# Attention masks on tiles of TensorE's array, shorter runs for the stack loads, late weights in pairs

## The chip, the cores and the metric

The kernel runs on one core of a Trainium2 chip. The time is the device time of one execution in microseconds, which is the time of the slowest core and here of the only one. TensorE (PE) multiplies, VectorE (DVE), ScalarE (ACT) and GpSimd (POOL) work on tiles, and SyncE (SP) issues nearly all transfers between memory (DRAM) and the on-chip memory (SBUF).

## The reference

A gated cross-attention block and a gated mixture of experts over 32 batches of 128 tokens with 128 features:

```python
x = x + tanh(g_xattn[0]) * attention(layernorm(x), ctx, ctx, mask, Wq, bq, ..., bo)
x = x + tanh(g_ffn[0]) * experts(layernorm(x), Wg, bg, Wt, bt, W1, b1, W2, b2)
# attention: 16 heads of 8 features
scores = einsum('bhqd,bhkd->bhqk', q, k) / sqrt(8)
scores = where(mask[:, None, :, :], finfo.min, scores)   # mask [b, q, k], one for all heads
out = softmax(scores) @ v @ Wo.T + bo
# experts: 8, all computed for every token
gate = softmax(x @ Wg + bg); thr = sigmoid(x @ Wt + bt) / 8
w = max(gate - thr, 0); w = w / sum(w)
out = sum_e w[:, e] * (gelu(x @ W1[e] + b1[e]) @ W2[e] + b2[e])
```

## The kernel before, in words

The kernel has two stages. The expert stage is the longer one and isn't part of the change. In the attention stage the 32 batches are handled in 16 groups of two. A loop written out over turns (`it`) works on several groups at once: `group_at(it, ahead)` tells which group a step handles in this turn, so that a turn holds the natural scores of group `it`, the transposed scores of the second batch of group `it - 1`, the head sums of that group, and so on. Each engine has its own program with the same turns, and its order is the order in which the code is written. Engines wait for each other by semaphores.

**Scores.** Queries and keys are kept in fp32 parts, stored to DRAM (`kq_scratch`) and read back as stacks (`kq_st`): four strips of 32 rows of the array (`ROWS`), each with 24 rows for one head at a time. For each batch TensorE makes the scores twice. The natural ones (queries on partitions, L1000) give DVE the row maxima (`neg_max`, L727). The maxima are turned by TensorE (max0 for the first batch, max1 for the second), copied by ACT (`maxT`) and sent by SP into two more rows of the stacks (L410, L418). The transposed ones (keys on partitions, L1025) then have the maxima taken off and go to ACT's exponentials (`probs`, L567). The values product (L1047) follows, with 32 columns of the array for each of four heads.

**Masks.** The mask of a batch, 128 x 128 bytes, is loaded as words with queries on partitions (`mask_words`, L360) and cast by POOL to bf16 (`mask_b`, L513). A matmul with a diagonal matrix of -2^126 (`masked_ident`) adds it to the scores: with the diagonal as weights for the natural ones (L983), with the mask as weights for the transposed ones (L1011). Each is a full matmul of 128 rows and 512 columns, that is one bank of PSUM with four heads. A batch has four banks each way. The masks of two banks make a pair, and the pair ends with the semaphore for which DVE or ACT waits; in the natural way banks 2 and 3 come first, then 0 and 1.

**After the values.** ACT copies the head sums (`headsT`), TensorE turns them, DVE divides (`merged`), TensorE turns again, ACT copies (`mergedT`), and the projection `wo` (L1124) follows. L1145 to L1147 are the projections to keys and queries, L1191 to L1193 those to values, L1204 the gate.

**SP's queue.** In a turn SP issues, in this order and each behind its own waits: the max1 rows (L410), the next mask and context (L360, L365), four stack loads of 192 KB (L377), the max0 rows (L418), expert weights and x (L386, L391), and four stores of keys and queries (L399, L403). In turn 0 `later_weights` adds six small loads behind that.

Of the kernel before, what the change touches and what calls it, by code (L numbers as in the profile page):

```python
# [85 lines left out]
def gated_block(nc, a):  # L86
# [3 lines left out]
    with ctx:  # L90
# [33 lines left out]
        mask_words = sa("mask_words", [P, 2, GB, S // 4], I32)  # L124
        mask_b = sa("mask_b", [P, 2, GB, S], BF16)
# [23 lines left out]
        merged = sa("merged", [P, 2, GB * H, HD], F32)  # L149
        mergedT = sa("mergedT", [P, 2, GT], F32)  # L150
# [4 lines left out]
        x2n = sa("x2n", [P, 2, GB, D], F32)  # L155
# [34 lines left out]
        kq_dram = nc.dram_tensor("kq_scratch", (NG, ROWS * 24, SLABS * 2 * GT), F32)  # L190
# [9 lines left out]
        bv_in = sem("bv_in")  # L200
        bias_in = sem("bias_in")
# [69 lines left out]
        N_WTS = 6 * 16  # L271
# [34 lines left out]
        def wait_spare_loads(eng):  # L306

            for u in range(2):
                eng.wait_ge(ctx_in[u], 8 * NG)
                eng.wait_ge(mask_in[u], 8 * NG)  # L310
                eng.wait_ge(w_in[u], 8 * NG)
# [10 lines left out]
        def _(sp):  # L322
            ctx_v = a["ctx"].rearrange("(g b p) d -> g p b d", p=P, b=GB)
            mask_v = a["mask"].rearrange("(g b) q k -> g q b k", b=GB)
# [13 lines left out]
            sp.dma_start(mask_words[:, 0, :, :], mask_v[0]).then_inc(mask_in[0], 16)  # L338
# [3 lines left out]
            def later_weights():  # L342

                sp.dma_start(bo_row[:], a["bo"].partition_broadcast(P)).then_inc(wts_in, 16)
                sp.dma_start(wo_sb[:], a["woT"]).then_inc(wts_in, 16)
                sp.dma_start(wg_sb[:], a["wg"]).then_inc(wts_in, 16)
                sp.dma_start(bg_row[:], a["bg"].partition_broadcast(P)).then_inc(wts_in, 16)
                sp.dma_start(b1_sb[:], a["b1"]).then_inc(wts_in, 16)
                sp.dma_start(b2_sb[:], a["b2"]).then_inc(wts_in, 16)

            def rows_of(g, c):
                return kq_dram[g].rearrange("(r c d) (s x) -> c (d s) r x", r=ROWS, c=3, s=SLABS)[c]
# [52 lines left out]
            def body(it):  # L405
# [19 lines left out]
                elif it == 0:  # L425
                    later_weights()
# [912 lines left out]
```

## Time and profile before

| | us |
|---|---|
| median of 3 runs | 620.04 (617.59 to 621.89) |
| the profiled execution: its time | 622.03 |
| its span in the trace | 620.2 |

| engine | busy us | share |
|---|---|---|
| PE | 593.7 | 96% |
| DVE | 479.4 | 77% |
| ACT | 378.2 | 61% |
| POOL | 178.8 | 29% |

### The profile page before, as it was taken

How to read it: one execution, taken by the hardware profiler on the slowest of the kernel's cores; microseconds unless marked ns; L12 is line 12 of the kernel's file. 1: busy time of each engine (PE TensorE's matmuls, PEld its weight loads, DVE VectorE, ACT ScalarE, POOL GpSimd, SP SyncE). 2: the span in 40 equal slices, each digit the busy share in tenths (PEclk: the TensorE clock that was granted, in tenths of full speed). 3: DMA queues.
4: the chain of work that ended last, by engine and by line, in shares of the span. 5: the costliest groups of instructions: out<-in, count | busy, mean ns of one | idle time of the engine just before them, and what ended most of it. 6: DMA issues, size and time to landing. Idle time of an engine off the chain costs nothing.

```text
span 620.2 us, 13793 instructions
## 1 busy us (share of the span) xinstructions
PE 593.7 (96%) x4504; PEld 451.6 (73%) x4504; DVE 479.4 (77%) x940; ACT 378.2 (61%) x625; POOL 178.8 (29%) x224
## 2 busy tenths in 40 slices
PE   7888999999999998999999999999999999999998
PEld 6655666666666655788878788787887887887886
DVE  3464777777777766588788889888888888888886
ACT  3143555555655545867776767676777676776773
POOL 7523444454552221212203212212112112122121
PEclk9997999999999989999999999999999999999999
DMA  6765654555655420051111211121121121121210
GB/s 184 200 157 139 177 176 146 143 162 159 164 150 160 144 55 5 6 103 51 45 58 35 66 58 52 51 65 42 45 68 51 36 65 51 51 64 38 68 51 17
DMA packets 43998, 55.12 MB, mean 89 GB/s; under 512 B 9520, under 2 KB 27824, under 8 KB 42416
## 3 DMA queue, kind: packets, MB, share of 16 engines
q1 hardware_dynamic: 43504, 53.99, 30.8%
q8 instruction: 29, 0.48, 0.3%
q10 hardware_dynamic: 448, 0.53, 0.2%
q14 instruction: 17, 0.14, 0.1%
HBM read 39.16 MB, written 14.81 MB: 87 GB/s over the span
## 4 chain that ended last, share of the span: by engine, by line
PE 85%; ACT 4%; DVE 3%; DMA 2%; SPq 2%; issue 2%; ACTq 0%; DVEq 0%
PE ps_h L1069 10%; PE ps_h L1071 9%; PE ps_h L1070 9%; PE ps_y L1084 9%; PE ps_y L1086 9%; PE ps_y L1085 9%; PE misc L1047 5%; PE scores L983 5%; PE scores L1011 3%; PE scores L1000 3%; PE scores L1025 3%; ACT probs L567 2%; PE misc L1124 2%; PE misc L1216 1%; PE misc L974 1%
## 5 line engine op out<-in xcount | busy, mean ns | idle before, releaser
L591 ACT ACTIVATE h_sb<-ps_h,b_sb 128x512 f32<-128x512 f32 x256 | 175.9, 689 | 102.2 <-PE ps_h L1071 92.2
L750 DVE TENSOR_TENSOR h_low<-h_sb,h_high 128x512 fp32r<-128x512 f32 x256 | 164.6, 683 | 0.1
L530 POOL TENSOR_TENSOR yT<-yT,weighted 128x512 f32<-128x512 f32 x54 | 70.8, 1311 | 277.8 <-DVE weighted L925 277.8
L746 DVE CAST h_high<-h_sb 128x512 fp32r<-128x512 f32 x128 | 97.8, 764 | 52.6 <-ACT h_sb L591 52.4
L727 DVE TENSOR_REDUCE neg_max<-scores 128x8 f32<-128x1024 f32 x64 | 78.0, 1222 | 48.0 <-PE scores L983 48.0
L1069 PE MATMUL ps_h<-x_high,w_high 128*128 (+1 forms) x256 | 101.8, 398 | 2.1 <-ACT h_sb L591 2.0
L1084 PE MATMUL ps_y<-h_high,w_high 128*128 128x512 f32 x256 | 100.2, 391 | 0.3 <-ACT h_high L595 0.3
L1071 PE MATMUL ps_h<-x_high,w_low 128*128 (+1 forms) x256 | 99.8, 390 | 0.0
L1070 PE MATMUL ps_h<-x_low,w_high 128*128 (+1 forms) x256 | 99.7, 390 | 0.0
L1086 PE MATMUL ps_y<-h_high,w_low 128*128 128x512 f32 x256 | 99.7, 389 | 0.0
L1085 PE MATMUL ps_y<-h_low,w_high 128*128 128x512 f32 x256 | 99.6, 389 | 0.0
L595 ACT ACTIVATE h_high<-ps_h,b_sb 128x512 fp32r<-128x512 f32 x128 | 87.2, 681 | 0.0
L567 ACT ACTIVATE probs<-scores 128x1024 f32<-128x1024 f32 x64 | 62.9, 1006 | 17.3 <-PE scores L1011 17.3
L1069 PEld LDWEIGHTS ps_h<-x_high,w_high 128*128 128x128 f32 x256 | 48.1, 188 | 14.6 <-issue 4.7
L1084 PEld LDWEIGHTS ps_y<-h_high,w_high 128*128 128x128 f32 x256 | 48.0, 188 | 11.2 <-ACT h_high L595 0.7
L1071 PEld LDWEIGHTS ps_h<-x_high,w_low 128*128 128x128 f32 x256 | 48.0, 188 | 10.2
L1086 PEld LDWEIGHTS ps_y<-h_high,w_low 128*128 128x128 f32 x256 | 48.0, 188 | 10.2
L1085 PEld LDWEIGHTS ps_y<-h_low,w_high 128*128 128x128 f32 x256 | 48.1, 188 | 9.8
L1070 PEld LDWEIGHTS ps_h<-x_low,w_high 128*128 128x128 f32 x256 | 48.1, 188 | 9.3
L925 DVE SCALAR_TENSOR_TENSOR weighted<-ps_y,b_sb,w_row 128x512 f32<-128x512 f32 x55 | 41.0, 746 | 0.0
L983 PE MATMUL scores<-mask_b,masked_ident 128*128 128x512 bf16 x128 | 39.2, 392 | 0.0
L1011 PE MATMUL scores<-masked_ident,mask_b 128*128 128x512 bf16 x128 | 35.8, 389 | 0.0
(127 smaller groups left out, 719.8 us busy)
## 6 DMA issues: line engine op xcount, KB each, us to landing
w_row<-w_scratch SPq DMA_DIRECT2D x64, 256.0 KB, 3.1
kq_st<-kq_scratch SPq DMA_DIRECT2D x64, 192.0 KB
kq_scratch<-kq_parts SPq DMA_DIRECT2D x30, 256.0 KB, 2.9
w_raw<-in_w_ffn SPq DMA_DIRECT2D x16, 256.0 KB, 2.9
kq_scratch<-kq_parts SPq DMA_DIRECT2D x32, 128.0 KB, 2.7
ctx_sb<-in_ctx SPq DMA_DIRECT2D x16, 128.0 KB, 3.2
out_y<-y_out SPq DMA_DIRECT2D x7, 256.0 KB, 2.3
x_all<-in_x SPq DMA_DIRECT2D x13, 128.0 KB, 3.5
```

What stands on the lines that cost most here:

```text
L567: nc.scalar.activation(probs[:, b, half * 8 * S:(half + 1) * 8 * S], scores[:, 2 + 2 * half:4 + 2 * half, :].rearrange("p r x -> p (r x)") ...
L591: nc.scalar.activation(h_sb[:, j % HBUF, :], ps_h[:, j % 4, :], ACT.Gelu_apprx_tanh, bias=b1_sb[:, j:j + 1]).then_inc(h_done, 1)
L595: nc.scalar.activation(h_high[:, j % HBUF, :], ps_h[:, j % 4, :], ACT.Gelu_apprx_tanh, bias=b1_sb[:, j:j + 1]).then_inc(high_even, 1)
L727: nc.vector.tensor_reduce(neg_max[:, b, rows, :], scores[:, rows, :].rearrange("p r (s k) -> p r s k", k=S), AX.X, ALU.max, negate=True).t ...
L746: nc.vector.tensor_copy(h_high[:, j % HBUF, :], h_sb[:, j % HBUF, :]).then_inc(high_odd, 1)
L750: nc.vector.tensor_tensor(h_low[:, j % HBUF, :], h_sb[:, j % HBUF, :], h_high[:, j % HBUF, :].bitcast(F32), ALU.subtract).then_inc(low2_do ...
L1069: mm(dst, w_high[:, e, cols], xh, start=True, stop=False)
L1070: mm(dst, w_high[:, e, cols], xl, start=False, stop=False)
L1071: mm(dst, w_low[:, e, cols], xh, start=False, stop=True).then_inc(h_full, 1)
L1084: mm(dst, w_high[:, E + e, cols], h_high[:, j % HBUF, :], start=(f == 0), stop=False)
L1085: mm(dst, w_high[:, E + e, cols], h_low[:, j % HBUF, :], start=False, stop=False)
L1086: mm(dst, w_low[:, E + e, cols], h_high[:, j % HBUF, :], start=False, stop=(f == FC - 1)).then_inc(w2_done, 1)
```

## The change

**Masks.** A DMA for each batch now loads the mask once into each of the four strips: partition i of a strip holds queries 4i to 4i+3 with 128 keys each (512 bytes). So that query order fits, the turned inputs, and headsT on the way back, are dealt (query 4i+j goes to place 32j+i). A natural pair is now eight matmuls, each of 32 rows and 32 columns of the array with 512 moving columns. A transposed pair is eight matmuls of 32 rows and 128 columns of the array with 128 moving columns. `mask_words` has one buffer in place of two, and its load moves from the turn two ahead to the turn one ahead. To make room, `merged`, `mergedT` and `x2n` have one buffer each.

**Matmuls without meaning.** `keep_busy` adds four full matmuls of 512 columns a turn; their results are overwritten.

**Transfers.** `kq_scratch` gets 16 words of padding behind each slab, so that a stack load reads four runs of 2 KB a row, where it read one of 8 KB. The six late weights come in three pairs, in turns 0, 2 and 6, with semaphores of their own.

```diff
-        mask_words = sa("mask_words", [P, 2, GB, S // 4], I32)
-        mask_b = sa("mask_b", [P, 2, GB, S], BF16)
+        mask_words = sa("mask_words", [P, GB, S], I32)
+        mask_b = sa("mask_b", [P, 2, GB, 4, S], BF16)
...
-        kq_dram = nc.dram_tensor("kq_scratch", (NG, ROWS * 24, SLABS * 2 * GT), F32)
+        kq_dram = nc.dram_tensor("kq_scratch", (NG, ROWS * 24, SLABS, 2 * GT + 16), F32)
...
+            def load_mask(g):
+                for b in range(GB):
+                    every = bass.AP(a["mask"].tensor, (g * GB + b) * 32 * S, [[0, ROWS], [S, 32], [1, S]])
+                    sp.dma_start(mask_words[:, b, :], every).then_inc(mask_in[g % 2], 16)
...
-            def later_weights():
...
+            def later_weights(it):
+                if it == 0:
+                    sp.dma_start(bo_row[:], a["bo"].partition_broadcast(P)).then_inc(wts_in, 16)
+                    sp.dma_start(wo_sb[:], a["woT"]).then_inc(wts_in, 16)
+                elif it == 2:
...
+                elif it == 6:
...
-                if (g := group_at(it, 2)) is not None:
-                    u = g % 2
+                if (g := group_at(it, 1)) is not None:
                     if g > 0:
-                        wait_count(sp, mask_done, g - 1)
-                        sp.dma_start(mask_words[:, u, :, :], mask_v[g]).then_inc(mask_in[u], 16)
+                        sp.wait_ge(mask_done, g)
+                        load_mask(g)
...
-                        sp.dma_start(kq_st[32 * r:32 * r + 24, g % 3, :, :, :].rearrange("p s n t -> p (s n t)").bitcast(F32),
-                                     kq_dram[g, 24 * r:24 * r + 24, :]).then_inc(kq_in[g % 3], 16)
+                        sp.dma_start(kq_st[32 * r:32 * r + 24, g % 3, :, :, :].rearrange("p s n t -> p s (n t)").bitcast(F32),
+                                     kq_dram[g, 24 * r:24 * r + 24, :, 0:2 * GT]).then_inc(kq_in[g % 3], 16)
...
-                    nc.gpsimd.tensor_copy(mask_b[:, u, :, :], mask_words[:, u, :, :].bitcast(U8)).then_inc(mask_done, 1)
+                    nc.gpsimd.tensor_copy(mask_b[:, u, :, :, :].rearrange("p b j k -> p b (j k)"), mask_words[:].bitcast(U8)).then_inc(mask_done, 1)
...
-                    nc.scalar.activation(headsT[:, 0, :], misc[:, bank_of("V0"), 0:2 * P], ACT.Copy).then_inc(misc_read[bank_of("V0")], 1)
+                    nc.scalar.activation(headsT[:, 0, :].rearrange("p (k i j) -> p k j i", k=2, j=4),
+                                         misc[:, bank_of("V0"), 0:2 * P].rearrange("p (k j i) -> p k j i", k=2, j=4), ACT.Copy).then_inc(misc_read[bank_of("V0")], 1)
...
-            def natural_mask(r, b, u):
-                return mm(scores[:, r, :].rearrange("p (s k) -> p s k", s=SLABS), masked_ident[:],
-                          mask_b[:, u, b, :].unsqueeze(1).to_broadcast([P, SLABS, S]), start=False, stop=True)
+            def keep_busy(bank, n, u):
+                for _ in range(n):
+                    mm(scores[:, bank, :], masked_ident[:], mask_b[:, u, 0, :, :].rearrange("p j k -> p (j k)"), start=True, stop=True)
+
+            def natural_mask(pair, b, u):
+                for j in range(4):
+                    for r in pair:
+                        rows = slice(32 * r, 32 * r + 32)
+                        ins = mm(scores[32 * j:32 * j + 32, r, :].rearrange("p (s k) -> p s k", s=SLABS), masked_ident[rows, rows],
+                                 mask_b[rows, u, b, j, :].unsqueeze(1).to_broadcast([32, SLABS, S]), start=False, stop=True)
+                return ins
...
-            def transposed_mask(r, b, u):
-                return mm(scores[:, 2 + r, :].rearrange("p (s q) -> p s q", s=SLABS), mask_b[:, u, b, :],
-                          masked_ident[:].unsqueeze(1).to_broadcast([P, SLABS, S]), start=False, stop=True)
+            def transposed_mask(pair, b, u):
+                for j in range(4):
+                    for r in pair:
+                        rows = slice(32 * r, 32 * r + 32)
+                        ins = mm(scores[:, 2 + r, :].rearrange("p (s j i) -> p j s i", s=SLABS, j=4)[:, j], mask_b[rows, u, b, j, :],
+                                 masked_ident[rows, rows].unsqueeze(1).to_broadcast([32, SLABS, 32]), start=False, stop=(j == 3))
+                return ins
...
+                if (g := group_at(it, 0)) is not None:
+                    wait_count(pe, tr_rest_read, 2 * g)
+                    keep_busy(5, 2, g % 2)
...
+                if (g := group_at(it, 0)) is not None:
+                    pe.wait_ge(nat_rest_read, 2 * g + 2)
+                    keep_busy(0, 1, g % 2)
...
+                if (g := group_at(it, 0)) is not None:
+                    keep_busy(0, 1, g % 2)
```

TensorE, the second half of a turn, before: the values product of the second batch (L1047), its rest of the natural masks (L983), the values projection, the transposed scores of the first batch (L1025) with their masks (L1011), the gate (L1204) and the turn of the head sums (L1216).

```order
L1047 MATMUL misc<-probs,v_pad 32x128 x16
L983 MATMUL scores<-mask_b,masked_ident 128x512 x2
L1191 MATMUL misc<-wv_high,inT_high 128x128
...
L1025 MATMUL scores<-kq_st 128x128 x16
L1011 MATMUL scores<-masked_ident,mask_b 128x512 x4
L1204 MATMUL misc<-wg_sb,x2T_sb 128x9 x2
L1216 MATMUL misc<-ident_sb,headsT 128x128 x4
```

The same piece in the changed kernel (L1009 and L1040 are the masks, L1002 is `keep_busy`):

```order
L1075 MATMUL misc<-probs,v_pad 32x128 x16
L1009 MATMUL scores<-mask_b,masked_ident 32x512 x8
L1002 MATMUL scores<-mask_b,masked_ident 128x512 x2
L1222 MATMUL misc<-wv_high,inT_high 128x128
...
L1055 MATMUL scores<-kq_st 128x128 x16
L1040 MATMUL scores<-masked_ident,mask_b 128x4x32 x16
L1002 MATMUL scores<-mask_b,masked_ident 128x512
L1240 MATMUL misc<-wg_sb,x2T_sb 128x9 x2
L1002 MATMUL scores<-mask_b,masked_ident 128x512
L1254 MATMUL misc<-ident_sb,headsT 128x128 x4
```

Two full masks became eight small ones, four became sixteen, and four full matmuls without meaning stand at three places of this half; the first half of the turn has none.

SP, from the stores of turn 0 to the max0 rows of turn 1, before:

```order
L403 DMA kq_scratch<-kq_parts 32x4x512 x2
L344 DMA bo_row<-in_bo 128x128
L345 DMA wo_sb<-in_woT 128x128
L346 DMA wg_sb<-in_wg 128x9
L347 DMA bg_row<-in_bg 128x9
L348 DMA b_sb<-in_b 128x32
L349 DMA b_sb<-in_b 128x8
L410 DMA kq_st<-maxT 4x4x128 x2
L360 DMA mask_words<-in_mask 128x2x32
L365 DMA ctx_sb<-in_ctx 128x2x128
L377 DMA kq_st<-kq_scratch 24x2048 x4
L418 DMA kq_st<-maxT 4x4x128 x2
```

The same stretch now:

```order
L413 DMA kq_scratch<-kq_parts 32x4x512 x2
L353 DMA bo_row<-in_bo 128x128
L354 DMA wo_sb<-in_woT 128x128
L420 DMA kq_st<-maxT 4x4x128 x2
L333 DMA mask_words<-in_mask 128x1x128 x2
L375 DMA ctx_sb<-in_ctx 128x2x128
L387 DMA kq_st<-kq_scratch 24x4x512 x4
L428 DMA kq_st<-maxT 4x4x128 x2
```

Four issues left the stretch, and one mask load became two.

## Rows read from the trace of the kernel before

**Rows 1.** Three turns as stretches: us, busy us (instructions) by engine, PEclk, DMA share, GB/s

```profile
35.39:52.31 16.92, 13.46 (x167) 8.48 (x167) 8.38 (x18) 6.22 (x11) 7.33 (x13) 0.87 0.57 137
...
52.31:66.87 14.56, 13.65 (x173) 8.88 (x172) 10.06 (x25) 6.86 (x12) 2.88 (x4) 0.92 0.52 140
...
121.63:135.29 13.66, 13.30 (x179) 8.91 (x179) 10.53 (x30) 7.55 (x14) 6.37 (x10) 1.00 0.56 160
```

**Rows 2.** TensorE's timeline in one settled turn: start us, us, operation, count [wait]

```profile
121.63 0.67 PE L1000 MATMUL scores<-kq_st 24*128 24x128 f32 x16
...
122.23 0.61 PE L983 MATMUL scores<-mask_b,masked_ident 128*128 128x512 bf16 x2
...
122.67 0.38 PE L974 MATMUL misc<-ident_sb,merged 128*128 128x128 f32 x2
...
123.62 0.68 PE L1124 MATMUL misc<-wo_sb,mergedT 128*128 128x128 f32 x4
...
124.23 1.08 PE L1047 MATMUL misc<-probs,v_pad 128*32 128x128 f32 x32
...
128.81 0.67 PE L1000 MATMUL scores<-kq_st 24*128 24x128 f32 x16 [0.28 <-ACT probs L567]
...
130.96 0.61 PE L983 MATMUL scores<-mask_b,masked_ident 128*128 128x512 bf16 x2
...
131.62 0.30 PE L1191 MATMUL misc<-wv_high,inT_high 128*128 128x128 f32 x1
...
133.00 1.04 PE L1011 MATMUL scores<-masked_ident,mask_b 128*128 128x512 bf16 x4
...
133.88 0.58 PE L1204 MATMUL misc<-wg_sb,x2T_sb 128*128 128x9 f32 x4
```

**Rows 3.** The same timeline, other engines

```profile
122.13 0.42 DVE L804 TENSOR_TENSOR merged<-misc,sums_r 128x256 f32<-128x256 f32 x1
...
123.09 0.38 ACT L610 ACTIVATE mergedT<-misc 128x256 f32<-128x256 f32 x1 [0.22 <-PE misc L974]
...
127.67 1.91 ACT L567 ACTIVATE probs<-scores 128x1024 f32<-128x1024 f32 x2
...
127.78 1.11 SPq L418 DMA_DIRECT2D kq_st<-maxT  x2
...
131.09 0.38 ACT L662 ACTIVATE headsT<-misc 128x256 f32<-128x256 f32 x1 [1.52 <-PE misc L1047]
```

**Rows 4.** Chain of waits that ends at 48.37: start us, us, what

```profile
34.73 0.43 SPq L346
...
36.37 0.43 SPq L349
...
39.15 1.75 SPq L377
...
42.74 5.59 DMA kq_st<-maxT
```

**Rows 5.** TensorE's timeline behind that chain

```profile
48.37 1.12 PE L1025 MATMUL scores<-kq_st 26*128 26x128 f32 x16 [2.79 <-DMA kq_st<-maxT]
```

**Rows 6.** Groups by line, settled turns: busy us, mean ns of one

```profile
L513 POOL CAST mask_b<-mask_words 128x256 bf16<-128x256 uint8 x11 | 4.4, 396 | 0.0
```

**Rows 7.** Instructions of one line: ns min/median/max, first and last start

```profile
L545 ACT ACTIVATE wqk_high<-probs x2: 438/442/447, 7.2 to 7.5; 128x128 fp32r<-128x128 f32 x2
```

**Rows 8.** Two stretches of 1 us, columns as in rows 1

```profile
127.00:128.00 1.00, 0.98 (x6) 0.39 (x5) 0.97 (x4) 0.59 (x3) 0.60 (x1) 1.00 0.69 164
...
134.00:135.00 1.00, 0.99 (x9) 0.78 (x8) 1.00 (x5) 0.67 (x1) 0.00 (x0) 1.00 1.01 383
```

**Rows 9.** One stretch, and TensorE's timeline in it

```profile
224.00:228.00 4.00, 3.22 (x50) 2.07 (x50) 1.23 (x1) 1.54 (x2) 3.53 (x5) 0.66 0.11 23
...
224.78 0.69 PE L1000 MATMUL scores<-kq_st 24*128 24x128 f32 x16 [0.92 <-ACT probs L567]
...
226.36 1.94 PE L1047 MATMUL misc<-probs,v_pad 128*32 128x128 f32 x32
```

More of the change, by code:

```diff
@@ L148, in gated_block @@
         sums_r = sa("sums_r", [P, GB * H], F32)
-        merged = sa("merged", [P, 2, GB * H, HD], F32)
-        mergedT = sa("mergedT", [P, 2, GT], F32)
+        merged = sa("merged", [P, GB * H, HD], F32)
+        mergedT = sa("mergedT", [P, GT], F32)
         x_biased = sa("x_biased", [P, GB, D], F32)
@@ L154, in gated_block @@
         rstd2 = sa("rstd2", [P, 2, GB], F32)
-        x2n = sa("x2n", [P, 2, GB, D], F32)
+        x2n = sa("x2n", [P, GB, D], F32)
         x2T = sa("x2T_sb", [P, 2, GT], F32)
@@ L556, in first_low_stores @@
             def first_low_stores():
-                rows = kq_dram[0].rearrange("(r c d) (s x) -> c (d s) r x", r=ROWS, c=3, s=SLABS)
+                rows = kq_dram[0].rearrange("(r c d) s x -> c (d s) r x", r=ROWS, c=3)[:, :, :, 0:2 * GT]
                 misc_wait_read(act, "kq", 0)
@@ L607, in body @@
                     misc_wait_full(act, "merged", g)
-                    if g >= 2:
-                        misc_wait_full(act, "wo", g - 2)
-                    nc.scalar.activation(mergedT[:, u, :], misc[:, bank_of("merged"), 0:GT], ACT.Copy).then_inc(misc_read[bank_of("merged")], 1)
+                    if g >= 1:
+                        misc_wait_full(act, "wo", g - 1)
+                    nc.scalar.activation(mergedT[:], misc[:, bank_of("merged"), 0:GT], ACT.Copy).then_inc(misc_read[bank_of("merged")], 1)
                 if (g := group_at(it, -3)) is not None:
@@ L661, in body @@
                         misc_wait_full(act, "heads", g - 1)
-                    nc.scalar.activation(headsT[:, 1, :], misc[:, bank_of("V1"), 0:2 * P], ACT.Copy).then_inc(misc_read[bank_of("V1")], 1)
+                    nc.scalar.activation(headsT[:, 1, :].rearrange("p (k i j) -> p k j i", k=2, j=4),
+                                         misc[:, bank_of("V1"), 0:2 * P].rearrange("p (k j i) -> p k j i", k=2, j=4), ACT.Copy).then_inc(misc_read[bank_of("V1")], 1)
                     if g == NG - 1:
@@ L801, in body @@
                     dve.wait_ge(recip_done, g + 1)
[L802 to L804 removed]
+                    if g >= 1:
+                        misc_wait_full(dve, "merged", g - 1)
+                    nc.vector.tensor_tensor(merged[:], hv[:, :, 0:HD], sums_r[:].unsqueeze(2).to_broadcast([P, GB * H, HD]),
                                             ALU.mult).then_inc(misc_read[bank_of("heads")], 1)
@@ L873, in body @@
                     dve.wait_ge(rstd2_done, g + 1)
-                    if g >= 2:
-                        misc_wait_full(dve, "x2T", g - 2)
+                    if g >= 1:
+                        misc_wait_full(dve, "x2T", g - 1)
                     for b in range(GB):
-                        nc.vector.tensor_scalar(x2n[:, u, b, :], x_all[:, g * GB + b, :],
+                        nc.vector.tensor_scalar(x2n[:, b, :], x_all[:, g * GB + b, :],
                                                 mean_var2[:, u, b, 0:1], rstd2[:, u, b:b + 1], ALU.subtract, ALU.mult).then_inc(x2n_done, 1)
@@ L973, in turn @@
                 for b in range(n):
-                    ins = nc.tensor.transpose(misc[:, k, b * S:(b + 1) * S], src(b), ident[:])
+                    out = misc[:, k, b * S:(b + 1) * S]
+                    ins = nc.tensor.transpose(dealt(out) if b >= GB else out, src(b), ident[:])
                 ins.then_inc(misc_full[k], 1)
@@ L1102, in body @@
                     misc_wait_read(pe, "heads", g)
-                    turn("merged", g, lambda b: merged[:, u, b * H:(b + 1) * H, :].rearrange("p h d -> p (h d)"))
+                    turn("merged", g, lambda b: merged[:, b * H:(b + 1) * H, :].rearrange("p h d -> p (h d)"))
                 if (g := group_at(it, -3)) is not None:
@@ L1108, in body @@
                         pe.wait_ge(g_copied, 1)
-                    turn("x2T", g, lambda b: x2n[:, u, b, :])
+                    turn("x2T", g, lambda b: x2n[:, b, :])
                     if g == NG - 1:
@@ L1123, in body @@
                     for b in range(GB):
-                        ins = mm(misc[:, bank_of("wo"), b * D:(b + 1) * D], mergedT[:, u, b * S:(b + 1) * S], wo_sb[:], start=True, stop=True)
+                        ins = mm(misc[:, bank_of("wo"), b * D:(b + 1) * D], mergedT[:, b * S:(b + 1) * S], wo_sb[:], start=True, stop=True)
                     ins.then_inc(misc_full[bank_of("wo")], 1)
```

50 lines of the change are left out of this document (23 added, 27 removed).

## The prediction

> **What bounds the kernel now.** I read the times by turn first (a turn is one step of the loop over groups), then TensorE's timeline in one settled turn, then the engines it waits for, and last the chain of waits in the one turn that is longer. A settled turn lasts 13.66 us, and TensorE is busy for 13.30 of it; DVE, ACT and POOL are busy for 10.53, 7.55 and 6.37 [rows 1]. There are 16 groups and some 15 such turns, and the expert stage behind them isn't touched. So the attention stage is TensorE's, with one exception: the turn from 35.39 to 52.31 lasts 16.92 us and the one behind it 14.56 [rows 1].
>
> Not all of TensorE's time counts. Its row at 128.81 shows a 0.28 us wait for ACT's exponentials, which run from 127.67 to 129.58 [rows 2, 3]. Projection `wo` starts at 123.62, just behind ACT's copy mergedT, which ends at 123.47; that copy follows the turn of `merged` (122.67), which itself follows DVE's product (it ends at 122.55) [rows 2, 3]. The values projection at 131.62 starts just behind ACT's headsT (ends at 131.47), though the masks before it began at 130.96 and need only 0.44 [rows 2, 3]. In those three places a quicker mask gives TensorE a longer wait, and no time.
>
> **Prices.** A pair of full mask matmuls takes 0.44 us (122.23 to 122.67), so one of 512 columns takes 0.22, and that is also the price of each matmul without meaning [rows 2]. A turn has eight such pairs, 16 matmuls.
>
> *Transposed pair, now 8 matmuls of 128 columns on two strips.* The nearest row is the sixteen products of kq_st on four strips, 0.60 us or 38 ns each (121.63 to 122.23), so 0.30 for eight [rows 2]. From below, four in a row on each strip at a quarter of 0.22 make 0.22. Those of kq_st load fp32 weights and the mask's are bf16, so I take 0.28.
>
> *Natural pair, now 8 matmuls of 512 columns on 32x32 tiles.* No row shows such tiles. The values product shows that column tiles do overlap: 32 matmuls in 1.08 us, 34 ns each [rows 2]. If each of the eight starts 38 ns behind the last, the pair takes 7 x 0.038 + 0.22 = 0.49; if they start together, 0.22 and a little. The start distances of both rows hold a weight load and a stream on one strip, which eight separate tiles don't share, so I take the middle, 0.36, and keep 0.25 and 0.49.
>
> The Trainium skill (TensorE: Matmul & The Clock Gate, "Measured speedup vs the span model") has tiles start 4 ns apart, which would make this pair 0.25; no row here shows that. The Trainium skill (TensorEngine Tiling (Array Packing), "Key Properties") also says that a change of the tiling mode drains TensorE. That speaks against the change, since every natural pair now enters and leaves a mode of its own; by it the pair goes to the upper end.
>
> **The sum for a turn.**
> - Rest of the natural masks for the second batch with two matmuls without meaning: 0.36 + 0.44 = 0.80, in place of the 0.66 from 130.96 to 131.62 in which 0.22 was waiting: +0.14.
> - Transposed masks of the first batch (133.00 to 133.88): 0.56 in place of 0.88: -0.32. The two meaningless matmuls around the gate: +0.44. The wait for nat_rest_read ahead of them costs nothing: DVE's second maximum follows the first, and TensorE has the values projection and 32 matmuls in between.
> - Next natural pair: -0.08.
> - Masks between `merged` and `wo`: 0, hidden by mergedT as above.
> - First transposed pair of the second batch: -0.16, since the max0 transpose, ACT's copy and its exponentials hang on it. The second pair: 0; the wait at 128.81 grows instead.
> - Natural pair behind the products at 128.81: -0.08.
>
> That is -0.06 a turn, -0.9 us over 15. What is saved in the masks goes into the four meaningless matmuls. With both upper prices it is about +0.3 a turn (+4.5), with both lower ones, where DVE's merged and ACT's exponentials stop some of it, -0.4 (-6).
>
> *Edits off the path.* POOL's cast of the mask has four times the elements, and 0.40 us for 256 [rows 6] makes at most 1.6 for 1024; POOL is busy for 6.37 of 13.66 us [rows 1] and hides it. If that cover went, SP would stand before the next mask load, with the stack loads and the max0 rows behind it. ACT's headsT writes now step through memory: wqk_high, a copy in such steps, takes 0.44 us for 128 columns against headsT's 0.38 for 256 [rows 3, 7]. Even 0.35 us more ends inside the two meaningless matmuls. The single buffers (merged, mergedT, x2n) wait for readers that are done most of a turn earlier: 0.
>
> *The long turn.* The two long turns hold 16.92 + 14.56 - 2 x 13.66 = 4.2 us more than settled ones [rows 1]. The products at 48.37 waited 2.79 us for the max0 rows, and ran at half rate (1.12 us for what takes 0.67 elsewhere) [rows 2, 4, 5]; the granted clock of the turn is 0.87 on average [rows 1], so after the wait it fell from 2.4 to 1.2 GHz for a while. The chain shows why the rows were late: SP issues without a pause, among it four late weights (34.73 to 36.80, 2.07 us); a stack load's issue then sticks for 1.75 us, and max0's rows need 5.59 us to land behind the stacks [rows 4]. The change takes those four issues out and adds one, a second mask load (like those, 0.43 us). Stack loads are read at 164 GB/s with 0.69 of the engines' time, 238 GB/s for a full share, while a stretch of shorter runs shows 383 at 1.01, or 379 [rows 8]; so 768 KB in 2 KB runs needs some 1.2 us less. With about 1.6 us from SP and 1.2 from the runs, the 2.79 us wait is covered, and with it goes what made the clock fall. I take 4.2; the bounds are 0 and 5.
>
> *Sum:* -4.2 - 0.9 = -5.1 us. Against the profiled execution's own 622.0 us that is 616.9. The median of the three runs, 620.0, lies 2.0 lower, so the forecast is **615 us**.
>
> **The rivals.**
>
> *The clock falls more often (slower).* Sixteen full-array matmuls a turn become four, and the rest uses part of the array. That the clock is near its limit in this stage shows from 224 to 228 us: granted 0.66 on average, after a wait of only 0.92 us for ACT, with the values product at 1.94 us in place of 1.08 [rows 2, 9]. One such stretch costs 0.86 us there and as much again in its neighbours, 1.5 in all. In a settled turn it holds at 1.00 now [rows 1]; the change thins out just the part from the second batch's transposed product to the natural one, with no meaningless matmul there. Three falls eat the gain; at one in every turn it is 615 + 15 x 1.5 = 637, in every other 626. Chance 0.17.
>
> *The tiles cost the lower price.* Then -4.2 - 6 gives 610. Chance 0.20. This is what the page's 4 ns would give.
>
> *The mask load holds up max0.* Its source now has an outermost size of 4. The Trainium skill (DMA: Bandwidth & Descriptors, "Rules for kernel authors") says that such a size confines a DMA to as many engines; no row tells engines apart. If so, each of four engines carries 32 KB more, at 383/16 = 24 GB/s 1.4 us [rows 8], ahead of the stacks and of max0's rows, issued from 127.78 to 128.89 and wanted 0.60 before the masks at 133.00 [rows 2, 3]. The shorter stack time of 1.2 us pays that back nearly. Where it doesn't, 0.5 us a turn makes 615 + 7 = 622. Chance 0.08.
>
> *Tiles of one strip don't overlap.* A natural pair is then four rounds of 0.22, 0.88; four pairs and the lost cover of mergedT make +1.9 a turn, 643. The values product speaks against it. Chance 0.05.
>
> *The forecast* has 0.50, with 610 to 620 around it.
>
> **Numbers.** About 1% (6.2 us) is what a measurement of this kernel tells from no change, so faster means under 613.8. Faster: 0.20 of the low price, 0.21 of the forecast, 0.41. Slower, over 626.2: 0.12 of the clock, 0.02 of the mask load, 0.05 of the tiles, 0.19. The same: 0.40. The range from 607 to 629 leaves out the ends of the clock's case and the tiles that don't overlap.
>
> **What would show it.** The wait before the transposed product of the second group gone, and its turn near 13.7 us; eight natural masks between 0.25 and 0.49 us from start to next start; the mask pair before max0 at 0.28; the products at 128.81 waiting longer for ACT; a clock of 1.00 in the settled turns. I am wrong if a settled turn differs from 13.66 by over 0.4 us, if TensorE waits for DMA rows in settled turns, or if the clock rows fall under 1.00 there.

## The result: slower by 3.7%, and where it shows

| | before | changed |
|---|---|---|
| median, us | 618.82 (616.83 to 621.89, 4 runs) | 640.88 (639.27 to 648.86, 4 runs) |
| profiled execution, us | 622.03 | 640.84 |
| its span, us | 620.2 | 639.0 |
| mean granted clock | 0.989 | 0.949 |

The ratio is 1.037 (95% interval 1.033 to 1.041): the change costs 22 us where a gain of 5 was forecast, and 640.9 lies outside the range of 607 to 629. All medians here and in the table of the experiments leave out runs that took over 1.5% longer than the fastest of the same kernel, which are two of the four of e2_runs8k and one each of e3_spread, e4_nokeep and e8_thick.

The granted clock of the changed kernel in the page's 40 slices, from the start, about 16 us each:

```profile
PEclk8898969978989958899999999999999999999999
```

The attention stage takes the first 17 slices. Ten of them are under 9, where the kernel before had two; behind them, in the expert stage, the clock is full as it was.

I read one turn of it that nothing disturbs, then a disturbed one. Columns as in [rows 1]; the first row is the undisturbed turn, the second a stretch that ends with a wait, the third what comes right behind it, the fourth the last turns:

```profile
93.18:106.30 13.12, 12.55 (x230) 9.12 (x231) 10.54 (x28) 8.05 (x15) 5.21 (x9) 1.00 0.48 142
...
66.00:79.84 13.84, 11.22 (x198) 7.87 (x195) 10.44 (x28) 8.06 (x14) 7.02 (x10) 1.00 0.69 166
...
79.80:90.00 10.20, 10.16 (x116) 7.20 (x117) 5.40 (x17) 4.02 (x7) 3.48 (x6) 0.55 0.42 120
...
220.00:240.00 20.00, 18.64 (x245) 13.81 (x246) 11.45 (x30) 7.77 (x15) 5.56 (x7) 0.60 0.43 115
```

**Undisturbed, a turn is quicker**: 13.12 us against 13.66 [rows 1], with TensorE busy for 12.55 in place of 13.30. Its timeline shows where (L1027 and L1055 are the natural and the transposed products, L1009 and L1040 their masks, L1002 the matmuls without meaning, L1222 the values projection, L1240 the gate):

```profile
93.18 0.67 PE L1027 MATMUL scores<-kq_st 24*128 24x128 f32 x16 [0.28 <-ACT probs L576]
93.78 0.41 PE L1009 MATMUL scores<-mask_b,masked_ident 32*32 32x512 bf16 x8
94.11 1.08 PE L1075 MATMUL misc<-probs,v_pad 128*32 128x128 f32 x32
95.13 0.41 PE L1009 MATMUL scores<-mask_b,masked_ident 32*32 32x512 bf16 x8
95.69 0.38 PE L1002 MATMUL scores<-mask_b,masked_ident 128*128 128x512 bf16 x1 [0.16 <-issue]
96.04 0.30 PE L1222 MATMUL misc<-wv_high,inT_high 128*128 128x128 f32 x1
...
96.82 0.67 PE L1055 MATMUL scores<-kq_st 26*128 26x128 f32 x16
97.33 0.41 PE L1040 MATMUL scores<-masked_ident,mask_b 32*128 32x128 bf16 x16
97.67 0.39 PE L1002 MATMUL scores<-mask_b,masked_ident 128*128 128x512 bf16 x1
97.89 0.57 PE L1240 MATMUL misc<-wg_sb,x2T_sb 128*128 128x9 f32 x4
98.31 0.38 PE L1002 MATMUL scores<-mask_b,masked_ident 128*128 128x512 bf16 x1
98.53 0.60 PE L1254 MATMUL misc<-ident_sb,headsT 128*128 128x128 f32 x4
```

From start to next start a natural pair takes 0.33 us (93.78 to 94.11; 0.39 where the turn of `merged` follows, 99.91 to 100.30), and two transposed pairs together 0.34 (97.33 to 97.67), where two full ones took 0.88 (133.00 to 133.88 [rows 2]). The eight records of a natural pair together last 0.41 us and one alone 0.385 (median), so all eight start within some 0.03 us of each other; the next work then follows 0.33 us after the first of them. Ahead of the values projection two matmuls without meaning are issued, and only the second has a record (95.69). The matmuls without meaning give back about half of what that saves.

**But few turns are undisturbed.** TensorE's waits in all of the changed kernel (us in total, times, longest):

```profile
PE scores L1055 <- DMA kq_st<-maxT: 11.1, 9, 2.1
PE scores L1027 <- ACT probs L576: 7.0, 16, 1.0
PE scores L1027 <- DMA kq_st<-kq_scratch: 3.5, 1, 3.5
```

and in the kernel before:

```profile
PE scores L1000 <- ACT probs L567: 6.8, 16, 0.9
PE scores L1025 <- DMA kq_st<-maxT: 3.1, 2, 2.8
PE scores L1000 <- DMA kq_st<-kq_scratch: 0.8, 1, 0.8
```

The one wait of 2.79 us for the maxima's rows [rows 5] isn't gone: ahead of the same product, the third transposed one, it is 2.07 us, although four of the late weights have left SP's queue there:

```profile
49.79 0.90 PE L1055 MATMUL scores<-kq_st 26*128 26x128 f32 x16 [2.07 <-DMA kq_st<-maxT]
```

Eight others for max0 rows stand across the stage, with a longer wait for the first stack at the start. One of them, and TensorE behind it:

```profile
79.84 0.67 PE L1055 MATMUL scores<-kq_st 26*128 26x128 f32 x16 [1.94 <-DMA kq_st<-maxT]
80.34 0.41 PE L1040 MATMUL scores<-masked_ident,mask_b 32*128 32x128 bf16 x16
80.68 0.96 PE L1002 MATMUL scores<-mask_b,masked_ident 128*128 128x512 bf16 x2
...
82.64 1.12 PE L1027 MATMUL scores<-kq_st 24*128 24x128 f32 x16
```

The products at 82.64 take 1.12 us for what takes 0.67 at 93.18: the clock went from 2.4 to 1.2 GHz after the wait, and the stretch from 79.8 to 90.0 has 0.55 on average. From one natural product of a second batch to the next (74.19 to 93.18) this turn needs 19.0 us, so with a wait of 1.94 us goes a loss of 5.9, the wait included.

SP's queue ahead of that wait:

```profile
67.45 1.20 SPq L420 DMA_DIRECT2D kq_st<-maxT  x2
68.70 1.14 SPq L333 DMA_DIRECT2D mask_words<-in_mask  x2
69.89 0.48 SPq L375 DMA_DIRECT2D ctx_sb<-in_ctx  x1
70.48 3.28 SPq L387 DMA_DIRECT2D kq_st<-kq_scratch  x4
73.86 1.17 SPq L428 DMA_DIRECT2D kq_st<-maxT  x2
```

and the same queue in a settled turn before:

```profile
123.23 0.44 SPq L360 DMA_DIRECT2D mask_words<-in_mask  x1
123.71 0.47 SPq L365 DMA_DIRECT2D ctx_sb<-in_ctx  x1
124.29 1.58 SPq L377 DMA_DIRECT2D kq_st<-kq_scratch  x4
```

From the mask load to the end of the stack loads SP now needs 5.1 us (68.70 to 73.76), before 2.6 (123.23 to 125.87): a second mask load, and 0.8 us for each stack load in place of 0.4. The max0 rows were issued from 73.86 and used 5.98 us later; before they were used, without a wait, 4.62 us after their issue (127.78 to 132.40, 0.60 before the masks at 133.00 [rows 2, 3]).

SP was late with them as well. ACT's copy of the maxima ended at 73.14, 0.72 us before SP came to issue them:

```profile
72.87 0.27 ACT L663 ACTIVATE maxT<-misc 32x128 fp32r<-32x128 f32 x1 [0.20 <-PE misc L1185]
```

In the kernel before it was nearly always SP that waited for this copy (first line, from 30 to 250 us), in the changed kernel it seldom was (second line):

```profile
SPq L418 <- ACT maxT L653: 28.4, 14, 4.3
...
SPq L428 <- ACT maxT L663: 8.4, 5, 2.7
```

### The profile page after: what moved, and what is told of

It is laid out like the page before. It is cut to its first block, busy times and chain, and to the rows that moved or that the text cites. A ratio compares the mean times of both kernels' runs of the same rounds, so it can differ in the third digit from the quotient of the medians.

```text
span 639.0 us, 15461 instructions
## 1 busy us (share of the span) xinstructions
PE 599.3 (94%) x5320; PEld 468.8 (73%) x5336; DVE 480.6 (75%) x940; ACT 386.6 (60%) x625; POOL 189.1 (30%) x224
## 4 chain that ended last, share of the span: by engine, by line
PE 56%; ACT 2%; issue 1%; DVE 0%; ACTq 0%; DVEq 0%
PE ps_h L1097 9%; PE ps_h L1099 9%; PE ps_h L1098 9%; PE ps_y L1112 9%; PE ps_y L1114 9%; PE ps_y L1113 9%; ACT h_sb L600 1%; PE misc L1075 1%; PE ps_t L1277 1%; PE ps_t L1299 0%; PE misc L1240 0%; ACT h_high L604 0%; ACT L600 0%; ACT L583 0%; PE scores L1055 0%
## 5 line engine op out<-in xcount | busy, mean ns | idle before, releaser
L1075 PE MATMUL misc<-probs,v_pad 128*32 128x128 f32 x1024 | 40.8, 308 | 0.5 <-issue 0.5
L1075 PEld LDWEIGHTS misc<-probs,v_pad 128*32 128x32 f32 x1024 | 30.3, 123 | 7.8 <-issue 5.8
```

The costliest lines, as they stand in the source:

```text
L1075: ins = mm(misc[32 * t:32 * t + 32, k_bank, k * P:(k + 1) * P], v_pad[:, u, b, h, :], probs[:, b, at:at + S], start=(o == 0), stop=(o == 1))
```

## The experiments

Each ran in three rounds beside the kernel before. "Waits" are those for `kq_st<-maxT`; PEclk is that of the stretch from 43 to 250 us. Both are read from the one profiled execution of each kernel; that of e5_moved, at 632.4 us, was the slowest of its four.

| kernel | median us | ratio (95%) | waits: us, times | PEclk |
|---|---|---|---|---|
| before | 618.8 to 620.2 | 1 | 3.1, 2 | 0.98 |
| changed | 640.88 | 1.037 (1.033 to 1.041) | 11.1, 9 | 0.87 |
| e1_noload | 625.48 | 1.010 (1.006 to 1.013) | 0.2, 1 | 0.92 |
| e2_runs8k | 648.42 | 1.048 (two runs, no interval) | 12.3, 8 | 0.84 |
| e3_spread | 651.98 | 1.049 (1.041 to 1.057) | 14.4, 8 | 0.83 |
| e4_nokeep | 657.64 | 1.066 (1.055 to 1.076) | 4.7, 4 | 0.78 |
| e5_moved | 626.93 | 1.011 (1.004 to 1.018) | 1.1, 1 | 0.87 |
| e6_engines | 630.09 | 1.016 (1.009 to 1.023) | 5.0, 5 | 0.88 |
| e7_before_late | 616.59 | 0.995 (0.993 to 0.998) | none | 0.99 |
| e8_thick | 636.50 | 1.022 (1.011 to 1.033) | 7.8, 11 | 0.95 |
| e9_filled | 612.04 | 0.990 (0.984 to 0.995) | 0.8, 2 | 1.00 |
| e10_filled2 | 614.02 | 0.990 (0.984 to 0.996) | 0.8, 1 | 0.98 |
| e11_before_runs2k | 620.74 | 1.002 (0.999 to 1.004) | 2.8, 5 | 1.00 |
| e12_filled8k | 612.12 | 0.989 (0.984 to 0.994) | 1.5, 2 | 0.98 |

### The mask loads left out

```diff
-                    if g > 0:
-                        sp.wait_ge(mask_done, g)
-                        load_mask(g)
+                    pass
```

> The changed kernel without the mask loads of groups 1 to 15 (every group is masked with group 0's words, so the output is another; POOL's cast and all matmuls stay). Theory M, the mask load holds up the max0 rows: the waits of TensorE for kq_st<-maxT (9 waits, 11.1 us in the changed kernel) fall under 2 us, the granted clock stays at 1.00 in the settled turns, and the time is 603 to 612 us. Theory S, the stack loads in 2 KB runs do it (0.79 us of SP for an issue in place of 0.37): only the 1.1 us that two mask issues take of SP come back, most waits stay, 628 to 640 us. Theory C, the thinner matmuls alone let the clock fall: waits go but the clock still falls, over 625 us.

The waits for the maxima's rows are gone, and 15.4 us with them. So the mask load makes them. But the 603 to 612 us of theory M were missed: the kernel is still slower than before, with a PEclk of 0.92. One stretch shows why, in the timeline and as windows:

```profile
162.90 0.67 PE L1024 MATMUL scores<-kq_st 24*128 24x128 f32 x16 [0.28 <-ACT probs L573]
163.50 0.44 PE L1006 MATMUL scores<-mask_b,masked_ident 32*32 32x512 bf16 x8
163.87 1.94 PE L1072 MATMUL misc<-probs,v_pad 128*32 128x128 f32 x32
```

```profile
156.00:163.00 7.00, 6.59 (x119) 4.77 (x120) 5.65 (x16) 5.13 (x11) 4.76 (x8) 1.00 0.42 108
163.00:167.00 4.00, 3.67 (x66) 2.48 (x67) 1.79 (x2) 1.28 (x2) 2.25 (x2) 0.59 0.92 256
...
205.00:240.00 35.00, 31.38 (x474) 22.46 (x468) 20.21 (x52) 13.73 (x23) 8.63 (x11) 0.70 0.20 56
```

No transfer holds TensorE up here. The only wait is the usual 0.28 us for ACT, and the values product takes 1.94 us in place of 1.08: the clock fell in a turn like all others, to 0.59 on average over 4 us. In the last turns it is at 0.70 over 35 us.

### The stack loads in runs of 8 KB again

```diff
-        kq_dram = nc.dram_tensor("kq_scratch", (NG, ROWS * 24, SLABS, 2 * GT + 16), F32)
+        kq_dram = nc.dram_tensor("kq_scratch", (NG, ROWS * 24, SLABS, 2 * GT), F32)
```

> The changed kernel with the stack loads as before, one run of 8 KB a row, no padding. Theory S: the four issues take 1.5 us of SP in place of 3.2, the waits for kq_st<-maxT go, 603 to 612 us. Theory M: the mask load still stands ahead of the max0 rows and the stack loads are slower in themselves, so the waits stay or grow, 638 to 655 us. Theory C: as now, 635 to 645.

Slower by 7.5 us in the medians (all four runs lie from 647.9 to 660.6, those of the changed kernel from 639.3 to 648.9), with a longest wait of 3.7 us in place of 2.1. With the mask load in the way the shorter runs help, though each of their issues costs SP twice as much. SP is in time again here: from 30 to 250 us it waits 13 times, 28.3 us in all, for ACT's copy of the maxima, as before. The waits for the rows stay all the same, so here the transfer makes them and not SP's issues.

### The mask load as four transfers, one for each strip

```diff
+                both = bass.AP(a["mask"].tensor, g * GB * 32 * S, [[S, 32], [32 * S, GB], [1, S]])
+                for r in range(ROWS):
+                    sp.dma_start(mask_words[32 * r:32 * r + 32, :, :], both).then_inc(mask_in[g % 2], 16)
```

> The changed kernel with the mask load cut into four DMAs by strip (32 partitions outermost, both batches in each) in place of two whose source begins with a step of 0 and a count of 4; same bytes and runs. Theory M with few DMA engines as its reason: waits for kq_st<-maxT fall under 3 us, 605 to 615 us, although SP has two more issues a turn. If it's the bytes or SP's time and not the engines, the time is 640 us or more.

It has 32 as outermost size, and two issues more. Waits went up to 14.4 us in all, and the 605 to 615 us were missed. This test alone doesn't tell the engines from the issues, which is why the engines got their own below. It does show that an outermost size of 32 by itself doesn't take the waits away.

### Without the matmuls without meaning

All four `keep_busy` of a turn are taken out.

> The changed kernel without the four full matmuls without meaning a turn. Where TensorE waits for the max0 rows anyway they cost little: theories M and S expect the waits to grow by up to 0.7 us each and the time to lie within 5 us of the changed kernel's 641. Theory C expects many more clock falls and over 650 us. If only their own time counted, 640.9 - 15 x 0.88 = 628 us.

The slowest of all, although it does the least work and waits only 4.7 us for the rows. PEclk is 0.78. The four matmuls cost 0.22 us each and are worth some 17 us here. Part of their own time isn't saved either: the values projection now waits for ACT's headsT 14 times, 6.2 us in all.

### The mask load moved to the end of SP's turn

```diff
-                if (g := group_at(it, 1)) is not None:
-                    if g > 0:
-                        sp.wait_ge(mask_done, g)
-                        load_mask(g)
...
+                if (g := group_at(it, 2)) is not None:
+                    if g > 0:
+                        sp.wait_ge(mask_done, g)
+                        load_mask(g)
```

> The changed kernel with the mask load of group it+2 issued at the end of SP's turn, behind the stores, in place of the load of group it+1 ahead of the context and the stacks. Same bytes, same two DMAs, same engines; only their place in SP's queue moves. Theory M in its form 'the mask load stands ahead of the stacks and the max0 rows': TensorE's waits for kq_st<-maxT fall from 11.1 us to under 3, and the time comes near the kernel without the loads (625.5): 622 to 630 us. If the bytes slow everything wherever they stand, the waits stay and it is 635 or more. Theory C (thinner matmuls) expects that also here the clock falls without a wait in late turns, as without the loads, and so no time under 620.

Nothing is left out here, and the load stands behind the stores. The time is that of the kernel without the loads (626.9 and 625.5), and one wait of 1.1 us is left of nine. The last 38 us of the stage, in this kernel:

```profile
212.00:250.00 38.00, 35.28 (x462) 25.47 (x460) 19.39 (x51) 13.96 (x23) 9.83 (x12) 0.59 0.21 58
```

Few stacks are left to load there (58 GB/s; the last load is issued at 226.1), TensorE waits for no transfer, and still the clock is at 0.59.

### The mask load from 128 outermost rows

```diff
-                    every = bass.AP(a["mask"].tensor, (g * GB + b) * 32 * S, [[0, ROWS], [S, 32], [1, S]])
+                    every = bass.AP(a["mask"].tensor, ((g * GB + b) % 28) * 32 * S, [[S, P], [1, S]])
```

> The changed kernel with a mask load whose source begins with 128 rows of 512 bytes in place of a step of 0 with a count of 4: the same two issues, bytes and runs, only not limited to few DMA engines (it reads other batches' mask bytes, so the output is another). If few engines are the reason within theory M: waits for kq_st<-maxT under 3 us and 622 to 630 us. If it is SP's time and the bytes: 636 to 645 us, as the changed kernel.

With the same bytes written, number of issues and place in the queue, the waits fall from 11.1 to 5.0 us and the time by 10.8. Both lie between the two expectations. So the form of the source decides over half of the waits. That fits the rule of the Trainium skill (DMA: Bandwidth & Descriptors, "Rules for kernel authors") by which an outermost size of 4 confines a transfer to at most as many engines; the traces don't tell engines apart, so the runs show an effect and not the engines. Two other things changed with the size. This source reads 64 KB once, where the changed kernel and e3_spread read the same bytes four times, and an issue takes SP 0.44 us in place of 0.56 (medians). Since e3_spread, with 32 outermost and two more issues, has the most waits of all, the size isn't shown to be the cause; no run reads each byte once from a small outermost size. The rest of the waits goes only when the load moves.

### Before, with the late weights in pairs

Only `later_weights` is taken over, with its semaphores.

> The kernel before with one part of the change alone: the late weights in three pairs. My prediction's step for the long turn expects the wait of 2.79 us before the transposed product of the second group and the clock fall behind it gone, 4 us faster: 614 to 616. If the stack loads' own time held the max0 rows, the wait stays above 1 us and the time within 1.5 us of before.

The ratio of 0.995 is a gain of 2.9 us (1.2 to 4.5), a little less than expected. No wait for the rows is left, and the products that had waited (then at half rate [rows 5]) start at 44.89 and take 0.67 us:

```profile
44.89 0.67 PE L1030 MATMUL scores<-kq_st 26*128 26x128 f32 x16
```

### The changed transfers with full masks

```diff
+                for r in pair:
+                    ins = mm(scores[:, r, :].rearrange("p (s k) -> p s k", s=SLABS), masked_ident[:],
+                             mask_b[:, u, b, 0, :].unsqueeze(1).to_broadcast([P, SLABS, S]), start=False, stop=True)
```

The transposed masks likewise, and no matmul without meaning. In this data all queries of a batch have the same mask, which is why the rows of one in four can stand for all.

> The changed kernel's transfers, casts and copies with full-array mask matmuls as before (two of 512 columns a pair, no meaningless ones; the mask is laid out for tiles, so the output is another). TensorE's order is that of the kernel before. Theory M: waits for kq_st<-maxT of 0.5 to 1.5 us in most turns. Theory C says that thick matmuls keep the clock up through waits of that size: low clock under 20 us in the attention stage, against 64 in the changed kernel, and 622 to 630 us. If the waits alone make the clock fall, 636 to 645.

Here are eleven waits, 7.8 us in all, and yet:

```profile
43.00:250.00 207.00, 188.40 (x2460) 127.66 (x2458) 144.70 (x372) 109.68 (x191) 87.15 (x121) 0.95 0.54 144
```

The longest wait, 1.54 us, leaves the next natural products at 0.67; one of 1.08 us later doesn't (153.28):

```profile
50.28 0.67 PE L1051 MATMUL scores<-kq_st 26*128 26x128 f32 x16 [1.54 <-DMA kq_st<-maxT]
...
52.69 0.67 PE L1025 MATMUL scores<-kq_st 24*128 24x128 f32 x16 [0.23 <-ACT probs L576]
...
62.92 0.30 PE L1215 MATMUL misc<-wv_high,inT_high 128*128 128x128 f32 x1 [0.29 <-ACT headsT L672]
...
149.80 0.67 PE L1051 MATMUL scores<-kq_st 26*128 26x128 f32 x16 [1.08 <-DMA kq_st<-maxT]
...
153.28 1.12 PE L1025 MATMUL scores<-kq_st 24*128 24x128 f32 x16
```

So full masks make the falls fewer and don't end them: the same stretch has 0.87 in the changed kernel and 0.95 here. But the time didn't follow. Theory C expected 622 to 630 us, and it is 636.5, some 20 us above the kernel with the late weights in pairs (616.6). My estimate of where they lie, from the two traces: 7.8 us in waits for the rows, 2.2 more before the first stack (3.5 against 1.3), 4.2 in 14 waits of the values projection for ACT's headsT (0.63 us in place of 0.38, as in the line at 62.92), and some 8 from the clock (0.95 against 0.99 over 207 us). With these transfers the tiles bring no gain: 640.9 (639.3 to 648.9) against 636.5 (628.8 to 640.4), though each undisturbed turn is 0.54 us shorter than before.

### The moved load, with TensorE's gaps filled

To the kernel with the moved load a full matmul is added just ahead of the second batch's natural product, where TensorE waits for ACT, and more in the last turns:

```diff
+                if it == NG:
+                    pe.wait_ge(nat_rest_read, 2 * NG)
+                    keep_busy(0, 5, 1)
...
+                if (g := group_at(it, 0)) is not None:
+                    pe.wait_ge(nat_rest_read, 2 * g + 1)
+                    keep_busy(0, 1 if g + 3 < NG else 4, g % 2)
```

> The kernel with the mask load moved to the end of SP's turn, and one more full matmul without meaning in TensorE's wait for ACT ahead of the second batch's natural product (four in the last three turns, which lack the input turns and wait 1.02 us there; five at the start of turn 16, which waits 1.19 us). Each fits into a wait of 0.28 us or 1.02 us. Theory C (the clock falls because too little of the array is at work around that wait, with no DMA wait needed): the four single falls in settled turns and the long ones behind 212 us go, low clock falls from 65 us to under 25, and the time is 608 to 616 us. If the falls hang on something else, it stays at 624 to 632.

```profile
43.00:250.00 207.00, 195.24 (x3485) 141.43 (x3516) 157.85 (x416) 127.51 (x222) 92.18 (x128) 1.00 0.53 144
...
212.00:250.00 38.00, 35.28 (x563) 25.74 (x566) 25.07 (x72) 24.57 (x43) 10.75 (x14) 1.00 0.10 25
...
110.55:123.66 13.11, 12.55 (x229) 9.20 (x232) 10.54 (x28) 8.04 (x15) 7.02 (x11) 1.00 0.62 169
```

The time falls by 14.9 us, to 612.0. The 38 us from 212 us, which stood at 0.59, stand at 1.00 (they hold later work here, since this kernel is ahead), and so does all from 43 to 250 us. A settled turn lasts 13.11 us, against 13.12 undisturbed in the changed kernel, so the added matmul costs nothing: it lies in the gap. It has no record of its own there, and the wait ahead of 110.55 still reads 0.28 us; the load of its weights has one:

```profile
110.00 0.10 PEld L1002 LDWEIGHTS scores<-mask_b,masked_ident 128*128 128x128 bf16 x1
```

This version beats both kernels, the one before by 1.0% (0.5 to 1.6).

A second one (and five in the last turns) brings no more. The 614.0 is the 2 us more that was expected, but the runs of the two kernels overlap (610.8 to 616.5 and 611.0 to 615.0):

> The same with two more matmuls a settled turn at that place, and five in the last turns. The second doesn't fit into the wait of 0.28 us and costs up to 0.16 us a turn, 2 us in all. If one was enough, it is 2 us slower than with one; if the clock still falls with one, it is faster, 606 to 614 us.

### The 2 KB runs by themselves

The padded scratch and its loads in the kernel before:

> The kernel before with one part of the change alone: the padded scratch and the stack loads in runs of 2 KB. My prediction took 1.2 us less for the stacks' transfer and nothing for SP, so a gain or nothing: 617 to 620 us. Theory S: an issue takes 0.79 us of SP in place of 0.37, 1.7 us a turn; with the mask load of 0.44 us the stacks are issued later, the max0 rows land later, and TensorE waits for them in some turns: 622 to 632 us.

No difference in time, and the 622 to 632 us of theory S were missed. But there is no gain in the transfer either. These are the queue's packets, MB and share of the engines' time from 56 to 220 us, in the kernel before and with 2 KB runs:

```profile
q1 hardware_dynamic: 19180, 25.12, 53.8%
...
q1 hardware_dynamic: 22507, 25.21, 57.1%
```

The same bytes take 3.3% of 164 us more, which over twelve turns is some 0.45 us a turn (my estimate). And the other way round, 8 KB runs in the best version:

> The version with the mask load at the end of SP's turn and TensorE's waits for ACT filled (612.0 us), but with the stack loads as before, one run of 8 KB a row. Theory: with the mask load out of the way the runs no longer matter for the max0 rows: four stack issues cost 1.6 us in place of 3.2, the transfer takes some 1.2 us longer, and no wait for kq_st<-maxT over 1 us appears in settled turns; 611 to 614 us. Rival: the 8 KB runs hold up the rows whatever SP does; then waits for them come back in several turns, the clock falls with them, and the time is 618 us or more.

612.12 against 612.04. With the mask load out of the way, the length of the runs is nothing to the time; with it in the way it was 7.5 us in the medians. Why the shorter runs help there, no run shows; padding and run length always change together.

## Why the prediction was wrong

**Prices of the tiles: the mechanism right, one size off, to the good.** The natural pair at 0.36 was right (0.33 to 0.34 ahead of the values product, 0.39 ahead of the turn of `merged`). The 4 ns from tile to tile of the Trainium skill (TensorE: Matmul & The Clock Gate, "Measured speedup vs the span model") agree with the trace, in which eight records last 0.41 us and one 0.385. What doesn't come out is the 0.25 for the pair: the next work starts 0.33 after the first of the eight, and what takes the 0.08 stays open. The transposed pair at 0.28 was dear: two take 0.34 where they stand together, 0.17 each, under the lower end of 0.22. By its terms the turn came to -0.06; it measured -0.54. The transposed scores of the first batch with their masks gave -0.63 in place of -0.32 (their products also went from 0.60 to 0.51, 96.82 to 97.33), the two meaningless matmuls around the gate cost 0.27 and not 0.44 (0.86 us from 97.67 to 98.53), and the two ahead of the values projection 0.25 and not 0.14. Over 15 turns these tiles alone would be -8 us. (With both upper prices the prediction's own terms make +0.39 a turn and not +0.3.)

**Off the path: right.** POOL's cast takes 1.04 us in place of 0.40, under the bound of 1.6; the only waits of POOL for a mask, two with 2.0 us, hold nobody up. ACT's headsT takes 0.63 us in place of 0.38 and is covered but for three waits, 1.0 us in all. The cover is the matmuls without meaning: without them it makes 14 waits of 6.2 us (e4_nokeep) or 4.2 us (e8_thick).

**The long turn: right for the late weights, wrong for the change.** In the kernel before, the 2.79 us wait went with the late weights alone, and they bring 2.9 us (1.2 to 4.5) where 4.2 stood. In the changed kernel 2.07 us of it are back ahead of the same product (49.79), so the sum's first term wasn't earned.

**The step that failed: "The shorter stack time of 1.2 us pays that back nearly."** It priced the mask load as 1.4 us on few engines against 1.2 us saved in the runs, and left 0.5 us a turn in the bad case, at a chance of 0.08. Measured: nine waits of up to 2.1 us, 11.1 in all, and 14 to 15 us of the time, since the kernels without the load or with it moved come to 625.5 and 626.9. The 1.2 us that were to pay for it aren't there. In the kernel before, 2 KB runs raised the engines' share of time from 53.8 to 57.1% and left the time as it was (ratio 1.002). The rate for shorter runs was read from 134 to 135 us [rows 8], when the last that SP had issued were two stores (at 132.62), and the stack loads show no such saving. What the sum left out besides stands in SP's rows: the price of a stack load's issue was taken over from a transfer with one run a row, and it doubled. That is 1.7 of the 2.4 us by which SP's part grew, and the second mask load is the rest. SP then issued the max0 rows 0.72 us after they were ready, ahead of the wait of 1.94 us. Cheap issues alone don't help, though: 8 KB runs are slower here (648.4) and equal in the best version. How the mask load's cost divides into SP's time, its bytes and the engines that it uses stays open.

**The second one: the clock was priced by itself.** One fall in every turn, at 637 us, was an end of a rival at 0.17, and the number is near what came; that is luck, since it holds clock falls alone, and 14 to 15 us of what was measured are the mask load's. But its trigger was looked for in the settled turn alone, and its price of 1.5 us a fall was that of a short one. The runs show both at once. The transfers make waits, and with tiles the clock falls more often: full masks with eleven waits keep 0.95, tiles with nine get 0.87, tiles without matmuls of no meaning 0.78. And it falls without any wait for a transfer too (e1_noload). With the load moved, the filled gaps give back another 14.9 us. So of the 29 us between the changed kernel (640.9) and the best (612.0), one half goes with the mask load's place and, behind that, the other with the clock. The two cases shouldn't have been added up as exclusive, since both came true. That each makes the other dearer isn't shown: no run fills the gaps with the load unmoved, and with full masks these transfers cost about 20 us, not less.

**What is left.** The forecast of 615 counts neither. The best version, which has neither, has 612.0, and 620.0 - 8.1 for the tiles - 2.9 for the weights + 2.7 for the longer wait at the start would be 611.7. That longer wait for the first stack (0.8 us before, 2.5 to 3.8 in all with the new mask load) stays open; no run took the first group's mask load away. Open too is what makes the clock fall at one gap of 0.28 us and not at the same gap a turn earlier.

## What to carry to other kernels

When matmuls get cheaper by using a part of the array, the time of a turn is no longer the only price: look at what the granted clock did in the trace after waits of that size, and put full matmuls into the gaps where the engine waits anyway, since there one cost nothing here. A load that gets bigger is put behind the ones that somebody waits for in that turn; the form of its source is worth a run too. A rate read from stores isn't taken for loads, nor the issue price of one run a row for four. And two risks on one path, a late transfer and a falling clock, are priced together.

## What the runs showed of the hardware

- Eight matmuls on 32x32 tiles with 512 columns each take 0.33 to 0.39 us to the next start, where one full one takes 0.22; the eight themselves start within some 0.03 us. Sixteen on strips of 32 rows with 128 columns each take 0.34, where four full ones took 0.88.
- A stack load of 24 rows costs SP's queue 0.80 us to issue with four runs of 2 KB a row (median of 64, changed kernel), and 0.36 with one run of 8 KB (kernel before), for the same 192 KB.
- Two mask loads of 64 KB a turn made 11.1 us of waits with a source of 4 outermost that reads its bytes four times, and 5.0 with one of 128 outermost that reads each byte once.
- The same stack loads took more of the engines' time in 2 KB runs (57.1%) than in 8 KB runs (53.8%).
- The clock fell to 1.2 GHz in a turn whose only wait was 0.28 us (e1_noload, 163.9 us), and was at 0.59 on average over the last 38 us of the stage (e5_moved); with full matmuls added in the gaps the stage from 43 us on had 1.00. From 212 to 250 us TensorE is busy for 35.28 of 38 us in both, so the busy share alone doesn't show the clock.
